# A graph network's second layer: nine node tiles gathered by index instead of seven, in a ring of five quads, with the tile loops written out

## What is computed

```python
def _L0_gnn_ref(node_features, edge_index, edge_features, W1, b1, W2, b2):
    tgt = edge_index[1]
    agg = jax.ops.segment_sum(edge_features, tgt, num_segments=N_NODES)
    counts = jax.ops.segment_sum(jnp.ones((edge_features.shape[0],), edge_features.dtype), tgt, num_segments=N_NODES)
    agg = agg / jnp.maximum(counts, 1.0)[:, None]
    combined = jnp.concatenate([agg, node_features], axis=1)
    h = jax.nn.relu(combined @ W1 + b1)
    return h @ W2 + b2

def _L1_gnn_ref(feat, src, dst, w_neigh, w_self, b_self):
    summed = jax.ops.segment_sum(feat[src], dst, num_segments=n)
    deg = jax.ops.segment_sum(jnp.ones_like(dst, dtype=feat.dtype), dst, num_segments=n)
    h_neigh = (summed / jnp.maximum(deg, 1.0)[:, None]) @ w_neigh.T
    return feat @ w_self.T + b_self + h_neigh

h = jnp.maximum(_layernorm(x, axis=-1), 0.0)
x = x + _L0_gnn_ref(h, edge_index, edge_attr_64, L0_gnn_W1, L0_gnn_b1, L0_gnn_W2, L0_gnn_b2)
h = jnp.maximum(_layernorm(x, axis=-1), 0.0)
return x + _L1_gnn_ref(h, src, dst, L1_gnn_w_neigh, L1_gnn_w_self, L1_gnn_b_self)
```

## Time and profile before

| what | value |
| --- | --- |
| median of 3 runs | 1198.36 us (1198.36 to 1198.54) |
| the profiled execution's own time | 1198.31 us |
| its span in the trace | 1196.4 us |
| mean granted TensorE clock | 0.981 of full speed |
| PE busy | 1125.3 us, 94% |
| DVE busy | 815.7 us, 68% |
| ACT busy | 520.3 us, 43% |
| POOL busy | 419.8 us, 35% |
| layer 0 with its keys | up to about 457 us of the span |
| layer 1 | from about 462 us to the end |

### The profile page before, as it was taken

One profiled execution on the slowest core, in us unless ns is written; L12 is line 12 of the kernel. 1 busy time (PEld: TensorE's weight loads), 2 busy tenths in 40 slices (PEclk: granted clock), 3 DMA queues, 4 the chain that ended last, 5 costly groups with the idle time before them and its releaser, 6 DMA issues.

```text
span 1196.4 us, 31423 instructions
## 1 busy us (share of the span) xinstructions
PE 1125.3 (94%) x11714; PEld 856.3 (72%) x11714; DVE 815.7 (68%) x1813; ACT 520.3 (43%) x987; POOL 419.8 (35%) x384
## 2 busy tenths in 40 slices
PE   3689999999979997999999999999999999999996
PEld 2677787778768886677677677767777777776774
DVE  6877787787762578677576766766757666676661
ACT  4435555333212465444344444444444444444441
POOL 3111111110006640545345354443634535353461
PEclk9899999999988998899999999999999999999998
DMA  7766655555551210212122121221212212121121
GB/s 245 236 195 202 187 158 158 158 158 160 165 192 49 77 58 18 71 58 76 47 65 67 58 70 53 61 61 53 78 48 66 62 53 71 51 70 58 54 78 32
DMA packets 66875, 116.15 MB, mean 97 GB/s; under 512 B 10463, under 2 KB 30643, under 8 KB 66781
## 3 DMA queue, kind: packets, MB, share of 16 engines
q1 hardware_dynamic: 51740, 75.12, 20.3%
q0 software_dynamic: 15040, 39.80, 11.9%
HBM read 101.93 MB, written 12.95 MB: 96 GB/s over the span
## 4 chain that ended last, share of the span: by engine, by line
PE 81%; DVE 7%; issue 4%; DVEq 3%; ACT 3%; DMA 2%; ACTq 0%; SPq 0%
PE bank L1176 35%; PE couples L1169 10%; PE couples L1008 8%; PE bank L1195 7%; PE bank L966 5%; PE bank L955 5%; PE bank L953 3%; PE couples L1013 2%; PE bank L1187 2%; PE bank L1207 1%; DMA kreg<-in_edge_attr_dram 1%; PE couples L922 1%; DVE oreg L1617 1%; ACT hbuf L677 1%; DVEq L1484 1%
## 5 line engine op out<-in xcount | busy, mean ns | idle before, releaser
L1176 PE MATMUL bank<-hreg,areg 128*128 128x512 f16 x2058 | 504.7, 382 | 0.0
L597 POOL DMA_INDIRECT wide<-h_table,aggn x280 | 324.8, 1160 | 408.8 <-PE couples L1169 194.1
L807 ACT ACTIVATE areg<-couples 128x784 bf16<-128x784 f32 x336 | 276.7, 824 | 369.7 <-PE couples L1169 367.5
L1176 PEld LDWEIGHTS bank<-hreg,areg 128*128 128x128 bf16 x2058 | 265.7, 144 | 104.5 <-issue 1.1
L1617 DVE TENSOR_TENSOR hids<-iota,kreg 128x1024 bf16<-128x1024 f16 x336 | 196.6, 626 | 48.8 <-PE couples L1169 48.7
L1617 DVE TENSOR_TENSOR oreg<-iota,kreg 128x1024 bf16<-128x1024 f16 x336 | 195.9, 624 | 46.2 <-PE couples L1169 44.8
L1008 PEld LDWEIGHTS couples<-oreg,kreg 128*64 128x64 f32 x3232 | 116.9, 142 | 63.8 <-issue 62.8
L1008 PE MATMUL couples<-oreg,kreg 128*64 128x48 f32 x3232 | 138.3, 230 | 20.3 <-DVE oreg L1369 14.7
L1369 DVE TENSOR_TENSOR oreg<-iota,wide 128x384 f32<-128x384 f32 x202 | 122.3, 606 | 4.4 <-issue 1.3
L564 POOL TENSOR_TENSOR xr<-xr,b2bc 128x512 f32 x25 | 33.2, 1326 | 224.9 <-ACT h0buf L687 224.9
L1169 PEld LDWEIGHTS couples<-oreg 128*128 128x128 bf16 x1344 | 76.8, 98 | 49.3 <-issue 13.6
(11 more groups left out here) (167 smaller groups left out, 1069.0 us busy)
## 6 DMA issues: line engine op xcount, KB each, us to landing
kreg<-in_edge_attr_dram SPq DMA_DIRECT2D x202, 256.0 KB, 2.7
h_table<-hreg SPq DMA_DIRECT2D x25, 256.0 KB
xr<-in_x_dram SPq DMA_DIRECT2D x6, 1024.0 KB, 7.5
out_dram<-hbuf SPq DMA_DIRECT2D x42, 128.0 KB
wide<-h_table,aggn POOLq DMA_INDIRECT x280
wide<-in_L_gnn_W_dram SPq DMA_DIRECT2D x2, 512.0 KB, 8.5
out_dram<-h0buf SPq DMA_DIRECT2D x6, 128.0 KB
hreg<-in_dst_dram SPq DMA_DIRECT2D x1, 512.0 KB
```

The source lines that it names most:

```text
L597: pool.indirect_dma_start(near[:, k, :], None, table, bass.IndirectOffsetOnAxis(ap=nearsrc[:, n * GHALF + k:n * GHALF + k + 1], axis=0)).t ...
L807: act.activation(step.rearrange("p (a k) -> p a k", a=2), cpl[s % 2][:, :, 0:BC * KEYS], ACT.Copy).then_inc(s_adj, 1)
L1176: ins = pe.matmul(bank[4 + par], adj[:, par, :, h], htab[:, h, :], start=(h == 0), stop=(h == TN - 1))
```

## The change

Nine tiles by index instead of seven, 40 dense tiles instead of 42. The blocks of keys are 20 instead of 21, in NK = 4 sets of KB = 5 instead of three of 7; the first set is computed in iteration 7 and transposed in iteration 8. A near tile has GC = 9 chunks, so 36 fetches and 36 products; the fullest window of 32 nodes in the inputs has 1135 edges and there is room for 1152. The fetches go into a ring of five quads (RING) of four buffers, a quad being the four windows of one chunk. The quads' sums are spread: `quad_step[n]` is the step after which TensorE sums quad n, and `finish[g]` the dense tile during which near tile g is finished (5, 9, 13, 17, 21, 25, 29, 33, 38). All loops over tiles in layer 1 are straight code for t = 0 to 39. The near tile's own steps stay at the places in a tile that they had.

```diff
-    KB = 7
-    PAUSES = 3, 6
-
-    GB = 4
+    KB = 5
+    PAUSES = 2, 4
+
+    GB = 5
...
-    GC = 10
+    GC = 9
...
+    PACE = 11
+    LANDED = 3
+    fetch_step = [k * 10 // PACE for k in range(GT * GC * WS)]
+    quad_step, finish = [], []
+    for g in range(GT):
+        free = (finish[-1] + 1) * ST + 1 if finish else 0
+        for c in range(GC):
+            quad_step.append(max(fetch_step[(g * GC + c + 1) * WS - 1] + LANDED, free))
+        finish.append(quad_step[-1] // ST + 1)
...
-                for n in range(BURSTS):
-                    if n > 0:
-                        pool.wait_ge(s_burst, n)
-                    for k in range(GHALF):
...
-                        pool.wait_ge(s_cplp, min((CYCLE // 2 * n + 1) * ST + k, DT * ST))
...
+                for k in range(GT * GC * WS):
+                    n, w = k // WS, k % WS
+                    if w == 0 and n >= RING:
+                        pool.wait_ge(s_burst, n - RING + 1)
+                    pool.wait_ge(s_cplp, ST + 1 + fetch_step[k])
...
+            def near_sums(n):
+
+                c, r = n % GC, n % RING
+                if c == 0 and n > 0:
+                    pe.wait_ge(s_res, place[DT + n // GC - 1] + 1)
+                pe.wait_ge(s_rows[r], 16 * WS * (n // RING + 1))
+                pe.wait_ge(s_onenear, n + 1)
+                for w in range(WS):
+                    ins = pe.matmul(bank[7][w * GW:(w + 1) * GW, :], onenear[:, r, w, :], near[:, r, w, :],
+                                    start=(c == 0), stop=(c == GC - 1))
                 ins.then_inc(s_burst, 1)
...
+                        for n, at in enumerate(quad_step):
+                            if at == t * ST + s:
+                                near_sums(n)
...
+                        for g in ends:
+                            if s == 7:
+                                result(DT + g, place[DT + g], 2, g or None, bank[7])
+                        for n, at in enumerate(quad_step):
+                            if at - 2 == t * ST + s:
+                                one_near(n)
```

More of the change, by code:

```diff
@@ L94, in gnn_kernel @@
     NK = DB // KB
-    CYCLE = 6
     GW = 32
-    GC = 10
+    GC = 9
     GR = 2 * (P // GW) * GC
-    GHALF = GC * (P // GW) // 2
-    BURSTS = 2 * GT
-    KEY0 = U // 2 - 3
+    WS = P // GW
+    RING = 5
+    BW = 7 * SL
+    STEPS = DT * ST
+    PACE = 11
[7 more added lines that the diff above has]
+        finish.append(quad_step[-1] // ST + 1)
+    order = []
+    for t in range(1, DT + 1):
+        order.append(t - 1)
+        order += [DT + g for g in range(GT) if finish[g] == t]
+    place = {t: m for m, t in enumerate(order)}
+    KEY0 = U // 2 - NK
     NOKEY = 1024.0
@@ L492, in result @@
                     sp.wait_ge(s_res, m + 1)
[L493 to L501, removed]
+                    sp.dma_start(out[t * P:t * P + n, :], finished[q][0:n, :]).then_inc(s_out[q], 16)
+                for m, t in enumerate(order):
+                    result(t, m, t % 2 if t < DT else 2, REST if t == TN - 1 else P)
                 sp.wait_ge(s_out[0], 16 * (DT // 2))
@@ L1139, in _ @@
             layer0(BESIDE)
[L1140 to L1141 removed]
+            for n in range(NK):
                 layer0(KEY0 + n, n)
@@ L1709, in one_near @@
                                       ALU.is_equal).then_inc(s_onenear, 1)
-                def tile(i, c, first=False, last=False):
-                    t, m, par = CYCLE * i + c, (CYCLE + 1) * i + c - 1, c % 2
-                    before = m - (c == 0)
+                for t in range(DT):
+                    par = t % 2
+                    ends = [g for g in range(GT) if finish[g] == t]
                     for s in range(ST):
-                        if not last:
+                        if t < DT - 1:
@@ L1728, in tile @@
-                        if s == 6:
-                            stored = CYCLE // 2 * i + (c - 1) // 2
-                            result(t - 1, before, 1 - par, stored if later(stored) else None, bank[5 - par])
-                        if c == 0 and s == 7:
-                            result(DT + i - 1, m, 2, i - 1 if not isinstance(i, int) or i > 1 else None, bank[7])
-                tile(0, 0, first=True)
-                for c in range(1, CYCLE):
-                    tile(0, c)
-                with dve.Fori(1, GT - 1) as i:
-                    for c in range(CYCLE):
-                        tile(i, c)
@@ L1740, in _ @@
-                for c in range(CYCLE):
-                    tile(GT - 1, c, last=(c == CYCLE - 1))
-                m = (CYCLE + 1) * GT - 2
-                sum_parts(DT - 1, m, s_dense, DT, bank[5])
-                result(DT - 1, m, 1, DT // 2 - 1, bank[5])
-                sum_parts(TN - 1, m + 1, s_burst, BURSTS, bank[7])
-                result(TN - 1, m + 1, 2, GT - 1, bank[7])
+                        if t > 0 and s == 1:
+                            sum_parts(t - 1, place[t - 1], s_dense, t, bank[5 - par])
@@ new lines, in _ @@
+                        for g in ends:
+                            if s == 3:
+                                sum_parts(DT + g, place[DT + g], s_burst, GC * (g + 1), bank[7])
+                        if t > 0 and s == 6:
+                            result(t - 1, place[t - 1], 1 - par, (t - 1) // 2 or None, bank[5 - par])
+                        for g in ends:
+                            if s == 7:
[3 more added lines that the diff above has]
+                                one_near(n)
```

172 lines of the change are left out of this document (64 added, 108 removed).

## The result

| | before | changed |
| --- | --- | --- |
| median of the runs | 1198.36 us (1196.68 to 1198.54, 4 runs) | 1185.51 us (1184.26 to 1185.83, 4 runs) |
| profiled execution's own time, span | 1198.31, 1196.4 us | 1184.26, 1182.5 us |
| ratio | | 0.9889, 95% interval 0.9877 to 0.9901 |

The change takes 1.1% away, 12.85 us of the median, where 10.8 us were forecast (1187.6 us, range 1177 to 1197). The profiled execution of the changed kernel is its fastest one, 1.25 us under its median, so the two traces differ by 13.9 us.

A forecast was written before the change was run, and what follows sets the result against it. PE's instruction order was taken as the bound. From 1198.3 us, -31.5 - 39.0 + 30.7 + 19.4 + 7.5 + 10.7 - 2.2 - 6.4 = -10.8 gave 1187.5, as a median 1187.6 us, range 1177 to 1197.

The forecast's parts named there:

- the two dense tiles: Layer 1 on PE: two dense tiles fewer at 15.77 us each, all on PE's path, -31.5 us.
- The price of a quad: Near products on PE: a lone quad lengthens its step by 0.42 us; 81 quads in 66 places, +30.7 us.
- The ends: Gaps on PE before and after near products, at changes between whole-array and quarter-array products: 0.20 us a place, +13.2 us.
- The first rival: Near products on PE: quads cost only the burst's mean, 0.256 us each, giving 1177.6 us; chance 0.12.
- the dear ends: Near products on PE: a lone quad's weight loads cannot hide, so end gaps double, +13.2 us, 1200.8 us; chance 0.10.
- The stalls: PE waits for VectorE at nine near-tile finishes: 0.83 us behind sums, +7.5; 0.65 behind results plus 23 `one_near`, +10.7 us.
- The body: Stretch from tile 1 to the last 25 dense products: 2.2 us shorter forecast.
- Fetches: 324 row fetches instead of 280 on GpSimd, landing in 2 to 4 us with over 6 us of cover: 0 us.
- The third rival: Ahead of each of 81 quads, rows land late and PE waits; 0.5 us each gives 1228 us; chance 0.06.
- turning point: Mean wait for rows ahead of each quad at which the change would turn slower: 0.16 us.
- The head: Key iterations before layer 1's tiles: PE's wait for VectorE's keys goes, four iterations take 73.2 against 75.7 us; -2.2 us.
- The tail: After the last dense tile: last near tile finished in tile 38, the store following either alike, -6.4 us.

The follow-up runs named there:

- the threes: Changed kernel with each quad summed when the last of its three is due, so 81 quads stand in 27 places instead of 66: 1178.76 us median.
- the whole-array products: Changed kernel with each near product made over 128 columns of constant weights, so near tiles' sums differ: 1229.13 us in a single run.
- the near sums a step later: Changed kernel with the near tile's sums on VectorE in step 4 instead of step 3: 1180.35 us median, ratio 0.9852 to the kernel before.
- two steps fewer: Changed kernel with LANDED = 1 instead of 3, every quad summed two steps sooner after its last fetch: 1198.85 us median, ratio 1.0002 to the kernel before.
- `one_near`: Changed kernel with every `one_near` operation one step later on VectorE: 1181.79 us median, ratio 0.9857 to the kernel before.
- near result: Changed kernel with VectorE's result of the near tile moved from step 7 to the next tile's step 0, behind its one-hots: 1177.05 us median.

## Why the prediction was right, point by point

**Which engine bounds, and the two dense tiles: right.** PE's order set the time: what an edit put into it or took out of it, waits for VectorE included, came back in the stretch, in the changed kernel and in the experiments.

**The price of a quad: right.** 0.42 us were forecast, 0.42 to 0.435 are measured. The ends are 0.22 and not 0.20 us a place, which is 1.3 us more over 66 places. The first rival (0.256 us a quad) and the dear ends (over 0.6) are both out: the threes show that the place is what costs, and the whole-array products show that it is the change of shape. The Trainium skill's rule in "TensorEngine Tiling (Array Packing)", Key Properties, that changing the mode drains TensorE, agrees: 0.22 us with the change, none without.

**The stalls: right in mechanism, a little too large.** The first is 0.79 us, not 0.83: the loop had 0.04 of it. It is still there in the kernel before without loops, and the near sums a step later make it go, in all nine tiles (7.1 us). The second was taken nine times, and there are eight: the ninth near tile is finished in tile 38, and tile 39 has no counts to come for which PE could wait. Its base is 0.57 us and a `one_near` is 0.2 us (four of them 0.81). Together 9.6 us instead of 10.7. Of these 0.35 stand at tile 17 alone: there VectorE's near result takes 0.85 us from its first operation to its second where it takes 0.50 elsewhere, with the label "issue" and no cause that a row shows.

**The body: 28 of 31.5 us given back.** The forecast had 29.3. With its quad in tile 0, which the table counts to the head, the body is -2.8 us where -2.2 was forecast; the stalls' 1.5 us too much and the ends' 1.3 us too little nearly cancel, which is luck, and 39.2 us were taken out where 39.0 were forecast. The loops' 1.2 us were in that sum nearly whole, because it was read off a cycle inside the loop; the prediction saw only 0.08 us a cycle of them, and put another 0.12 a near tile back in with the two stalls.

**Fetches: right.** No wait for rows, and landing takes 3.0 us in the median where 2 to 4 were forecast. But the cover is needed: two steps fewer cost 11.2 us. The third rival described the right mechanism; one constant in the change keeps it away. (Its turning point was too high: against 1198.4 us it is 10.8 / 81 = 0.13 us a quad, not 0.16.)

**The head: right.** Four iterations take 73.1 us together, against 73.2 forecast and 75.7 before; PE's wait for keys is gone. The stretch's 2.5 us contain one quad (+0.4). From iteration 12 to tile 1 the changed kernel needs 0.3 us less without that quad (39.66 - 0.43 against 39.54), which stays open. How close this came is partly luck: in the three experiments that leave the order of this stretch on PE alone (near sums, `one_near`, near result) it takes 113.4, 116.1 and 112.7 us. In the longest, iteration 11 takes 21.1 us instead of 18.1, because PE waits 2.22 us at 451.74 for ScalarE, which had waited for VectorE, at a granted clock of 1.00. So the clock is not the cause; VectorE's own wait (5.43 us, put down to "remote") is as far as the rows go.

**The tail: the step that failed in size.** "The store follows either alike" was wrong. The 6.4 us to the last result were right by construction, since they were read from the trace that was then compared, and they held 1.1 us of clock: in the trace of the kernel before without loops, where the last products ran at full granted clock, the same distance is 1186.79 - 1181.47 = 5.3 us. The remaining 2.1 us are in what comes after the last result. The kernel before stores the node tile of 106 rows last, and waits 3.6 us for it; the changed kernel does that tile in tile 38, ahead of two whole ones, and waits 1.8 us for 128 rows. The same wait is 3.6 us again in the kernel before without loops, and 1.8 to 2.1 in six experiments on the changed kernel. This is the largest single part of the 3.1 us by which the traces' difference exceeds the forecast.

## What to carry to other kernels

Price an insertion by the number of times the array's shape changes, not by its products: 81 quads cost 32 us in 66 places and 23 in 27. Before blaming a loop for idle time labelled "issue", look at the same wait elsewhere in the trace, which may name its releaser, and look which buffer the next instruction needs and who read it last. And look at what is queued behind a waiting instruction on an in-order engine, because moving it a step (nine sums, eight results) was worth more here (16.7 us) than the whole change (12.9). Let the last transfer of a kernel be one of a full tile where the order allows it; here 106 rows in one store cost 1.8 us more than 128.

## What the runs showed of the hardware that was not expected

The last store's 106 rows took twice as long as 128 rows (3.6 and 1.8 us of waiting); cut into 96 and 10 rows they took 1.3 us. The DMA view of the last microseconds counts packets under 512 bytes, which are not rows: 2 with the store of 106 rows, 16 with that of 128, and 26 with those of 96 and 10. If each DMA engine that takes part ends with one such packet, the 106 rows went over two of the sixteen engines. That is read from the counts and not shown directly; the busy share fits, since it stays at one or two tenths of the sixteen engines with 106 rows and reaches nine tenths with 128.

The change between products over 128 x 128 and over 128 x 32 costs 0.11 us each way on PE, and inside a group of quads there is no gap at all: four quarter products take the 0.216 us of a whole one.

At the end of the kernel before, the last four products ran at a granted clock of 0.50 (1.2 GHz, where full speed is 2.4). Beside them four such products some 5 us earlier, at full clock:

```profile
1183.21 1.03 PE L1195 MATMUL bank<-wss,hbuf 128*128 128x256 f32 x4
...
1188.72 1.91 PE L1195 MATMUL bank<-wss,hbuf 128*128 128x256 f32 x4
```

In the 9 us before them, since its dense products ended, PE had stood idle 0.69, 1.98 and 0.69 us. But the order doesn't decide it. The same tail with the same idle times ran at full clock in the trace without loops, and at half again in that with the cut-up store. The changed kernel's tail ran at full clock in its own trace and at half in those with the quads in threes and with the near result moved. Whether a tail falls into it changes its length by 1.1 to 1.3 us from execution to execution.
